# Four graph layers on one core: the last stage's two passes as one, a deeper gather ring in the segment maximum, and another engine to release adjacency slots

## The reference

```
xs, xd = x[src], x[dst]
reflection(a, b) = relu([a, b] @ W1.T) @ W2.T        # 32 -> 64 -> 16
F = I - 2 v v^T  with v = reflection / its norm      # one for (xs, xd), one for (xd, xs)
msg_s = coef * (-F_s^T F_d xd)   added to node src
msg_d = coef * (-F_d^T F_s xs)   added to node dst
out = relu(x - sum of msg_s by src - sum of msg_d by dst)
```

## Time and profile before

| | us |
|---|---|
| median of 3 runs | 8465.72 (8461.97 to 8473.73) |
| the profiled execution, its own time | 8461.1 |
| its span, first to last instruction | 8459.0 |

### The profile page before, as it was taken

How to read it: one execution, slowest core, us unless ns; L and a number is a source line. 1 busy time by engine, 2 the same in 40 slices (tenths; PEclk the granted TensorE clock), 3 DMA queues, 4 the chain that set the end, 5 groups by cost and what they waited for, 6 DMA issues and landing times. The chain is left out here.

```text
span 8459.0 us, 123102 instructions
## 1 busy us (share of the span) xinstructions
PE 5854.0 (69%) x33625; PEld 3950.5 (47%) x33626; DVE 6136.2 (73%) x12788; ACT 1635.2 (19%) x2872; POOL 4450.0 (53%) x4142
## 2 busy tenths in 40 slices
PE   3433333347444477777699999466559699999999
PEld 1333333236444455555455555255424366666555
DVE  5766666547333399999899999889900188888898
ACT  0011111001010144444222222034100022222000
POOL 0377767567777577777477777300000177777100
PEclk9999999955555599999899999677879755555899
DMA  2122222233111233333411111022065311111000
GB/s 97 32 52 53 52 51 52 43 108 70 38 36 38 37 79 80 80 80 79 54 44 43 43 44 43 13 94 99 31 253 205 148 31 32 32 32 32 3 0 1
DMA packets 487779, 514.79 MB, mean 61 GB/s; under 512 B 259365, under 2 KB 389805, under 8 KB 477106
## 3 DMA queue, kind: packets, MB, share of 16 engines
q1 hardware_dynamic: 344198, 446.65, 16.9%
q0 software_dynamic: 132160, 43.97, 6.5%
q10 hardware_dynamic: 11232, 21.73, 0.8%
HBM read 415.02 MB, written 95.99 MB: 60 GB/s over the span
## 5 line engine op out<-in xcount | busy, mean ns | idle before, releaser
L1257 POOL DMA_INDIRECT sh_ring<-node,sh_idx x832 | 856.8, 1030 | 1535.4 <-DVE sh_idx L1895 1277.6
L421 POOL DMA_INDIRECT slots<-rank_staged,rank_row_i x800 | 952.0, 1190 | 414.7 <-issue 210.1
L1507 POOL DMA_INDIRECT slots<-sm_rec,sm_row x832 | 900.9, 1083 | 361.8 <-issue 208.8
L1257 POOL DMA_INDIRECT mx_ring<-node,mx_idx x832 | 861.1, 1035 | 398.2 <-issue 239.5
L919 POOL DMA_INDIRECT mid_ring<-typed,mid_idx x832 | 873.5, 1050 | 258.7 <-issue 253.2
L401 PE MATMUL rank_found<-rank_next_sb,rank_hot_hi_t 25*125 25x128 f32 x1600 | 407.3, 431 | 840.3 <-ACT rank_next_sb L386 825.0
L1617 PE MATMUL sm_sums<-sm_both,sm_hot 128*128 128x512 f32 x1664 | 787.1, 595 | 0.4 <-issue 0.2
L401 PEld LDWEIGHTS rank_found<-rank_next_sb,rank_hot_hi_t 25*125 25x125 f32 x1600 | 353.6, 321 | 890.3 <-DVE rank_hot_hi_t L340 890.3
L1124 PE MATMUL mid_sums<-mid_ring,mid_hot_d 128*128 128x17 f32 x1664 | 391.7, 375 | 455.9 <-DMA mid_ring<-typed,mid_idx 443.5
L1124 PEld LDWEIGHTS mid_sums<-mid_ring,mid_hot_d 128*128 128x128 f32 x1664 | 383.3, 312 | 472.6 <-issue 472.6
L2135 PE MATMUL srl_sums<-srl_outer,srl_hot_lo 128*128 128x400 f32 x1664 | 560.9, 500 | 7.4 <-DVE srl_outer L2117 7.4
(11 more groups left out here) (403 smaller groups left out, 13634.0 us busy)
## 6 DMA issues: line engine op xcount, KB each, us to landing
strips<-near SPq DMA_DIRECT2D x76, 1600.0 KB, 10.8
mx_far<-far_row SPq DMA_DIRECT2D x208, 256.0 KB
rank_key_row<-key_rows SPq DMA_DIRECT2D x200, 244.1 KB
near<-adj_whole SPq DMA_DIRECT2D x175, 256.0 KB, 2.0
sm_low<-low_row SPq DMA_DIRECT2D x208, 128.0 KB
sh_low<-low_row SPq DMA_DIRECT2D x104, 256.0 KB, 3.3
feat_t<-mid_out ACTq DMA_DIRECT2D x104, 204.0 KB
mx_feat<-feat_t SPq DMA_DIRECT2D x208, 102.0 KB
```

Of the source, the lines that this page charges most:

```text
L421: pool.indirect_dma_start(m.slots, bass.IndirectOffsetOnAxis(ap=row_i[:, h, j:j + 1], axis=0), staged[:, h, j, :], None).then_inc(sent[h], 16)
L1257: pool.indirect_dma_start(ring[:, h, j, :], None, table, bass.IndirectOffsetOnAxis(ap=idx[:, h, j:j + 1], axis=0)).then_inc(part, 16)
L1507: pool.indirect_dma_start(m.slots2, bass.IndirectOffsetOnAxis(ap=row2[:, t:t + 1], axis=0), rec2[:, t, :], None).then_inc(ordered, 16)
```

## The change

The messages and the sums by source become one stage, `sheaf_messages`, of 52 turns of sixteen tiles (`MB`), rolled by a new helper `fours` over four turns. `to_sources` and `m.parts` are gone. The DVE one-hots of the node in its block are made in 16 bits with both operands in 16 bits, in pairs of tiles; the one for sources is widened to 32 bits by ACT (`widen`). The 32-bit product L2135 stays as it is, as `sources`, in two halves of eight tiles for each batch. `outer` now has one buffer for each half. The turned ends and the hidden layer go through PSUM in chunks of 512 columns, two buffers each. All gather indices are written at once, and the ring holds four batches; POOL's gathers are unrolled.

In the segment maximum the indices are written once and the ring holds four batches; PE's and ACT's loops cover four turns.

In the adjacency POOL loads the release counts, waits on `evac` and adds one to a new semaphore `freed` for each tile; PE waits on `freed` against a running count and loads eight table values a turn. `m.table` is laid out accordingly.

```diff
+MB = 16
...
+        @block.gpsimd
+        def _(pool):
+            def turn(q, h):
+                n = 2 * q + h
+                _, cleared_by = nc.values_load_multi_w_load_instructions(
+                    m.table[0:1, 1, bass.ds(n * BT, BT)], engines=[mybir.EngineType.Pool], min_val=0,
+                    max_val=(NB - 1) * (WIDTH_SLOTS + 1), skip_runtime_bounds_check_because=COUNTED)
+                for j in range(BT):
+                    pool.wait_ge(evac, cleared_by[j] & 511)
+                    pool.sem_inc(freed, 1)
+
+            batches(pool, total, 1, 1, turn)
+
...
                 _, at = nc.values_load_multi_w_load_instructions(
-                    m.table[0:1, bass.ds(n * BT, BT), :].rearrange("o t k -> o (t k)"), engines=[mybir.EngineType.PE], min_val=0,
+                    m.table[0:1, 0, bass.ds(n * BT, BT)], engines=[mybir.EngineType.PE], min_val=0,
                     max_val=(WIDTH_SLOTS - 1) * P, skip_runtime_bounds_check_because=COUNTED)
                 pe.wait_ge(hot_s, n + 1)
                 for j in range(BT):
-                    pe.wait_ge(evac, at[2 * j + 1] & 511)
+                    pe.wait_ge(freed, n * BT + j + 1)
                     for k in range(3):
-                        last = nc.tensor.matmul(sums[:, bass.ds(at[2 * j], P)], hot[:, h, j // 2, :, j % 2], heavy[:, h, k, j // 2, :, j % 2], start=False,
+                        last = nc.tensor.matmul(sums[:, bass.ds(at[j], P)], hot[:, h, j // 2, :, j % 2], heavy[:, h, k, j // 2, :, j % 2], start=False,
...
+def fours(eng, total, body):
+
+    for j in range(4):
+        body(0, j)
+    with eng.Fori(0, total - 2) as i:
+        for j in range(4):
+            body(i + 1, j)
+    for j in range(4):
+        body(total - 1, j)
+
...
     with ExitStack() as ctx:
         sb, ps, sem = makers(nc, ctx, "mx")
-        idx, ring = sb("idx", [P, 2, HB], I32), sb("ring", [P, 2, HB, W40])
+        idx, ring = sb("idx", [P, NT], I32), sb("ring", [P, DEEP, HB, W40])
...
         def _(pool):
-            gather(nc, m, pool, m.node40, idx, ring, idx_s, gathered, HB, HT // 2)
+            pool.wait_ge(idx_s, 1)
+            for n in range(HT):
+                if n >= DEEP:
+                    pool.wait_ge(held, n - DEEP + 1)
+                for j in range(HB):
+                    t = n * HB + j
+                    pool.indirect_dma_start(ring[:, n % DEEP, j, :], None, m.node40,
...
-                if inside(n + 2):
-
-                    dve.wait_ge(held, n + 1)
-                    indices(n + 2, h)
...
+                nc.scalar.copy(m.held[:, bass.ds(n * HB, HB), :], ring[:, k, :, 0:D]).then_inc(held, 1)
 
             def widened(n):
                 act.wait_ge(wide_s, n + 1)
...
-    total = NT // TB
...
+        idx, ring, low = sb("idx", [P, NT], I32), sb("ring", [P, DEEP, MB, HW]), sb("low", [P, 2, MB * P], FP16)
+        src_i, hi_i, lo_i = (sb(n, [P, NT], I32) for n in ("src_i", "hi_i", "lo_i"))
+        hi, real = sb("hi", [P, NT]), sb("real", [P, NT])
+        lo16, src16, iota = sb("lo16", [P, NT], BF16), sb("src16", [P, NT], BF16), sb("iota", [P, P, 2], BF16)
+        hot, hot_t = sb("hot", [P, 2, MB // 2, P, 2], BF16), sb("hot_t", [P, MB * P], BF16)
+        hot_s, hot_w, hot_hi = sb("hot_s", [P, MB // 2, P, 2], BF16), sb("hot_w", [P, 2, MB, P]), sb("hot_hi", [P, MB, NB])
+        outer = sb("outer", [P, 2, MB // 2, NB * D])
+        ends, ends_t, hid = sb("ends", [P, 2, MB, 2, D]), sb("ends_t", [2 * D, MB * P]), sb("hid", [P, MB * P])
...
+        xd, et_ps, hid_ps = ps("xd", [P, 512]), ps("et_ps", [2 * D, 2, 512]), ps("hid_ps", [P, 2, 512])
+        v_ps, sums, sums_f = ps("v_ps", [P, MB, 2 * D]), ps("sums", [P, 512]), ps("sums_f", [P, 512])
...
+            pool.wait_ge(idx_s, 1)
+            for n in range(total):
+                if n >= DEEP:
+                    pool.wait_ge(vec_s, n - DEEP + 1)
+                for j in range(MB):
+                    t = n * MB + j
+                    pool.indirect_dma_start(ring[:, n % DEEP, j, :], None, m.node20,
+                                            bass.IndirectOffsetOnAxis(ap=idx[:, t:t + 1], axis=0)).then_inc(gathered[n % DEEP], 16)
...
+
+            def far_hots(q, j):
+                n, h = 4 * q + j, j % 2
+                dve.wait_ge(loaded[h], (2 * q + j // 2 + 1) * 16)
                 wait(dve, xd_s, n)
                 nc.vector.tensor_scalar(hot_t[:, :], low[:, h], m.iota_col[:, 0:1], None, ALU.is_equal).then_inc(hot_t_s, 1)
...
+            def near_hots(n, h):
                 wait(dve, used, n - 1)
-                nc.vector.tensor_tensor(hot[:, h], slot_field(m, n * TB, TB, LO)[:, :, None].to_broadcast([P, TB, P]),
-                                        m.iota_row[:, None, :].to_broadcast([P, TB, P]), ALU.is_equal).then_inc(hot_s, 1)
...
+                nc.vector.tensor_tensor(hot[:, h], by_pairs(lo16, n), columns, ALU.is_equal).then_inc(hot_d_s, 1)
+                wait(dve, wide_s, 2 * n)
+                nc.vector.tensor_tensor(hot_s[:, :, :, :], by_pairs(src16, n), columns, ALU.is_equal).then_inc(hot_s_s, 1)
+
...
+                dve.wait_ge(v_s, 4 * n + 4)
+                link(nc.vector.tensor_tensor(flat(vec), v_ps[:, :, :], m.mlp_b2[:, None, :].to_broadcast([P, MB, 2 * D]), ALU.add))
                 link(nc.vector.tensor_tensor(sq[:, :, :, :], vec[:, :, :, :], vec[:, :, :, :], ALU.mult))
                 nc.vector.tensor_reduce(norm[:, :, :], sq[:, :, :, :], AX.X, ALU.add).then_inc(norm_s, 1)
                 if inside(n + 2, total):
-                    far_hots(q + 1, h)
+                    far_hots(q + (j + 2) // 4, (j + 2) % 4)
+                near_hots(n, h)
+                nc.vector.tensor_tensor(hot_hi[:, :, :], hi[:, bass.ds(n * MB, MB)][:, :, None].to_broadcast([P, MB, NB]),
+                                        m.iota_row[:, None, 1:NB + 1].to_broadcast([P, MB, NB]), ALU.is_equal).then_inc(chain, 1)
+                c[0] = c[0] + 1
...
                 if inside(n + 2, total):
-                    gather_ends(q + 1, h)
-
-            for h in range(2):
-                indices(h, h)
+                    gather_ends(q + (j + 2) // 4, (j + 2) % 4)
+                for k in range(2):
+                    t = slice(k * MB // 2, (k + 1) * MB // 2)
+                    wait(dve, spent, 2 * n - 1 + k)
+                    nc.vector.tensor_tensor(outer[:, k].rearrange("q t (s d) -> q t s d", d=D),
+                                            both[:, t, 0, :][:, :, None, :].to_broadcast([P, MB // 2, NB, D]),
+                                            hot_hi[:, t, :, None].to_broadcast([P, MB // 2, NB, D]), ALU.mult).then_inc(outer_s, 1)
...
+            def turned(n, c):
+                act.wait_ge(et_s, 4 * n + c + 1)
+                nc.scalar.copy(ends_t[:, c * 512:(c + 1) * 512], et_ps[:, c % 2, :]).then_inc(ends_t_s, 1)
+
+            def hidden(n, c):
+                act.wait_ge(hp_s, 4 * n + c + 1)
+                nc.scalar.activation(hid[:, c * 512:(c + 1) * 512], hid_ps[:, c % 2, :], ACT.Relu, bias=m.mlp_b1[:, 0:1]).then_inc(hid_s, 1)
...
+            def widen(n, h, k):
+                if k == 0:
+                    act.wait_ge(hot_s_s, n + 1)
+                    wait(act, spent, 2 * n - 2)
+                nc.scalar.copy(hot_w[:, h, k * MB // 2:(k + 1) * MB // 2, :].rearrange("q (a t) c -> q a t c", t=2),
+                               hot_s[:, k * MB // 4:(k + 1) * MB // 4, :, :].rearrange("q a c t -> q a t c")).then_inc(wide_s, 1)
...
                 act.wait_ge(norm_s, n + 1)
                 nc.scalar.activation(norm[:, :, :], norm[:, :, :], ACT.Sqrt).then_inc(root_s, 1)
-                if inside(n + 1, total):
-                    network(n + 1)
-                act.wait_ge(three_s, n + 1)
-                nc.scalar.copy(m.parts[:, bass.ds(n * TB, TB), :], both[:, h, :, 0, :]).then_inc(kept_s, 1)
-
-            network(0)
-            batches(act, total, 1, 1, turn)
+                if more:
+                    turned(n + 1, 0)
+                    turned(n + 1, 1)
+                    hidden(n + 1, 0)
+                    turned(n + 1, 2)
+                    hidden(n + 1, 1)
+                    turned(n + 1, 3)
+                widen(n, h, 0)
+                if more:
+                    hidden(n + 1, 2)
+                widen(n, h, 1)
+                if more:
+                    hidden(n + 1, 3)
...
+            def sources(n, h, k):
+                pe.wait_ge(outer_s, 2 * n + k + 1)
+                pe.wait_ge(wide_s, 2 * n + k + 1)
+                for j in range(MB // 2):
+                    last = nc.tensor.matmul(sums_f[:, 0:NB * D], hot_w[:, h, k * MB // 2 + j, :], outer[:, k, j, :], start=False, stop=True,
+                                            skip_group_check=True)
+                last.then_inc(spent, 1)
+
+            def turn(q, j):
+                n, h = 4 * q + j, j % 2
```

(43 more changed lines are left out.)

297 lines of the change are left out of this document (133 added, 164 removed).

## The result

| | us |
|---|---|
| before, median of 4 runs | 8463.84 (8461.23 to 8473.73) |
| after, median of 4 runs | 8633.15 (8623.0 to 8652.89) |
| ratio | 1.0201, interval 1.0181 to 1.0221 |
| profiled execution after: its own time, its span | 8652.89, 8651.1 |

What follows compares the result with a forecast made beforehand. PE was taken to bound both sheaf stages; merged, steps a to f sum to 34.7 us a turn, the stage +120 us. With segment maximum -79 and adjacency -18, 8461.1 became 8484, forecast as 8490 us, range 8400 to 8590.

Steps and rivals of the forecast that it cites:

- a: Merged turn's start: DVE's operations to the norms, then ACT's root and first copy, before PE's hidden layer starts; 3.0 us.
- f: Merged turn's end: DVE writes outer's second half only after PE's sources have counted it spent; 3.8 us.
- b: Merged turn, PE at 1.2 GHz up to the sources: hidden chunks, transposes, far-end products, vectors; 13.6 us.
- c: Merged turn, first half of PE's sources, eight tiles, the clock rising after 3.6 us; 7.2 us.
- d: Merged turn, PE's two groups of vectors between the halves of the sources; 1.7 us, or 3.2 if the clock isn't up.
- e: Merged turn, second half of PE's sources; 5.4 us.
- the rule of the Trainium skill: Rival in the merged stage: PE's busy time raises the clock 3.6 us into b; turn 27.9 us, kernel 8135, chance 0.05.
- the small parts bring nothing: Rival: the segment maximum and adjacency edits gain nothing; kernel 8490 + 80 = 8570 us, chance 0.07.
- Segment maximum, -79 forecast: Segment maximum: DVE's index write and waits for late gathers go; 208 turns of 5.40 us, 1123 us, -79 (-50 to -95).
- POOL's floor: Segment maximum: least turn POOL's gathers allow, 1.32 us a tile, 5.3 us for four; at the most -95 us.
- Adjacency, -18 forecast: Adjacency: halved table loads cut PE's late starts, the detour over POOL costs some; -18 us, from +15 to -45.
- issue time halved: Sign to look for in the adjacency: PE's issue time at the weight loads, 272.4 us before, should be halved.

Runs made afterwards that it cites:

- The experiment with full rows: Changed kernel with the hidden layer's weights and turned ends held in 128 rows, 96 of them zero: 8326.69 us, ratio 0.9838.
- the other kernels: Four kernels measured side by side with the changed segment maximum's code: that stage took 1152 to 1157 us in all.
- the kernel with both edits: Changed kernel with hidden-layer products over 128 rows and outer's second half written behind the next turn's norms: 8076.68 us, ratio 0.9547.
- the pieces: The kernel with both edits, each half of outer written by four DVE instructions of 800 elements: ratios 0.9647, 0.9647, 0.9434 on disturbed chips.

## Why the prediction was wrong

- **Which engine binds, and the order of the turn: right.** DVE's 22.3 us were 22.2, the waits a and f stand where they were put, and moving one of them gained 6.8 us a turn. It was no bar to the merge but a mistake in its order.
- **b, 13.6 forecast, 15.5 measured: mis-sized.** I took a hidden chunk as half the distance of two that followed each other, 1.85 us. In the merged order each stands between other products and takes 2.0, four times. Vectors took 1.83 instead of 1.6, twice; part of that is a reading, since I took the starts of weight loads, and the products' own starts in the old turn give (7214.55 - 7211.13) / 2 = 1.7. The far ends took 2.08 instead of 1.3, the largest error (0.8). The 0.64 a batch was no misreading; the products' own starts in the old turn say the same:

```profile
7210.48 0.81 PE L2020 MATMUL sh_xd<-wide,sh_hot_t 128*128 x24
7211.13 3.60 PE L2042 MATMUL sh_v_ps<-mlp,sh_hid 128*128 128x32 f32 x16
```

  What failed is doubling it. In the merged turn the first 26 of the 48 products also start 0.027 us apart; the rest come with pauses of about 0.1 us, 0.8 us in all. PE's program works out block addresses in register operations (FUSED_REGOPS in the trace), by their count one for two products, and 0.125 us apart. Nine of them are done when the products start, in the old order as in the merged one. The old batch needs three more, which come in time; the double batch needs fifteen more, and 15 x 0.125 = 1.9 us is nearly the 2.08 that the group takes. The transposes took 0.1 more. 0.6 + 0.5 + 0.8 + 0.1 is the missing 1.9 us, within rounding.
- **c, 7.2 forecast, 8.3 measured: mis-sized.** The clock came up after 5.7 us of sources, not 3.6. One rise was taken as the delay of all; it is a range. Steps d, e and f held to 0.1 us.
- **The price of a turn.** 52 x (37.24 - 34.7) = 132 us of the 139 that the stage missed by; filling and draining took 7 more. My range for the turn, 34.1 to 36.3, let only d, a and an earlier clock vary. None of the terms that failed had a bound of its own.
- **Rivals.** None came about. The clock did not come up in b, so the rule of the Trainium skill (TensorE: Matmul & The Clock Gate, What's actually happening), by which busy time releases it, gives 8135 where 8633 was measured: PE was busy without a break from 7417.6 on, and the clock came at 7438.8. The experiment with full rows says what the row of busy time leaves out: a PE that was no busier (85% against 88%) had 0.83 when its hidden products filled the rows. (The sum of the rival "the small parts bring nothing" leaves out the adjacency's 18 us; it should read 8587, not 8570.)
- **Segment maximum, -79 forecast, -20 in the profile, -53 in the kernel with the merge undone (1205 to 1152).** The mechanism held: the old waits for indices are gone, and POOL waits for next to nothing in the changed stage:

```profile
L1359 POOL DMA_INDIRECT mx_ring<-node,mx_idx x832 | 888.5, 1068 | 323.5 <-issue 248.4 <-DVE mx_idx L1388 69.3 <-ACT held L1399 5.9
```

  (The 69.3 lie ahead of the first gather.) Two terms were mis-sized. One is POOL's floor, 1.32 us a tile plus 0.1 a turn: the gathers follow each other with 0.30 us between, (888.5 + 248.4) / 832 = 1.37 us a tile, and the first 200 turns take 5.50 us each, where they took 5.66 before. In the other kernels it is 1.33 a tile and 5.34 a turn. The other is one pace for all turns. Near the end of the stage transfers of features come late to PE while the DMA engines are 91% busy (4040 to 4082; 34% in mid-stage): from the end of the 201st batch's gathers to the end of the stage it took 69 us before and 80 after. 200 x 0.16 - 11 is the 20 us of the profile, and 200 x 0.32 - 8 the 55 of the kernel with the merge undone. Nothing is hidden behind a deeper ring when the gathers themselves are the bound.
- **Adjacency, -18 forecast, -46 measured.** The gain lies at the far end of my range (-45), not where I put it. Every turn is now DVE's 3.22 us. PE's timeline before, then after (start, us):

```profile
5711.01 2.74 PE L679 MATMUL adj_sums<-adj_heavy,adj_hot 128*128 128x128 bf16 x24 [1.72 <-DVE adj_heavy L641]
5714.13 1.83 PE L679 MATMUL adj_sums<-adj_heavy,adj_hot 128*128 128x128 bf16 x24 [0.38 <-DVE adj_heavy L641]
5717.82 2.72 PE L679 MATMUL adj_sums<-adj_heavy,adj_hot 128*128 128x128 bf16 x24 [1.86 <-DVE adj_heavy L641]
```
```profile
5710.10 1.84 PE L694 MATMUL adj_sums<-adj_heavy,adj_hot 128*128 128x128 bf16 x24 [1.41 <-POOLq L677]
5713.35 1.81 PE L694 MATMUL adj_sums<-adj_heavy,adj_hot 128*128 128x128 bf16 x24 [1.41 <-DVE adj_heavy L643]
```

  Before, every other turn's 24 products took 2.7 us in this stretch, at half the clock; after, all take 1.8, and the granted clock is 0.98 where it was 0.81. I read the excess as load time and as waits for ACT, and did not look at the clock. The forecast sign "issue time halved" was wrong (276 us, as before), so the loads are not what was gained. Why the clock no longer falls is not settled: whether the detour over GpSimd does it, or the shorter work on PE's registers, was not separated.

## What to carry over

Before two stages are merged, ask which engine binds each: if it is the same one, merging saves nothing but the waits and the clock, and each new wait costs in full. Give every term of a serial sum its own bound, taken in the neighbourhood in which it will run, since a product alone between others took 2.0 us where two in a row took 1.85 each, and 48 small ones took more than twice what 24 did. And when two stages begin to overlap, look for operations that never ran beside each other before: here the long DVE write beside GpSimd's gathers set the next bound.

## What the runs showed of the hardware

- **A gather waits for the DVE instruction that runs.** One that starts beside a 3.49 us operation of two tensors takes up to 4.27 us and ends 0.82 us behind it at the median (98 of 124 in the kernel with both edits; the 26 that started within 0.043 us of its start were not held). Beside pieces of 0.9 us it takes at most 1.76, alone 0.94. With the pieces, 1 of 832 still waited for two DVE instructions in a row (3.14 us, in the first of three runs).
- **PE's register operations can hold small products.** One for two products, 0.125 us apart: a group of 48 pauses for 0.8 us behind its first 26 products (2.08 us in all; 3.3 in the turn shown of the kernel with both edits, where none of the 24 was done ahead); groups of 24, 0.65 us each, and of 12 hardly pause.
- **PE's busy share does not tell the clock.** It was 0.50 with PE busy from 7417.6 to 7438.8 (1.2 GHz, where 1.00 is 2.4). Zero rows added to the hidden layer's products (431 of PE's 1735 us in the stage) went with a mean of 0.83 instead of 0.68. With both edits it fell from 1.00 behind 3.3 us of far-end products; with these spread out, the mean of the stage with pieces was 0.89 instead of 0.83.
- **The rise is not at a fixed distance**: it came 3.6 us into the sums by source at one place and 5.7 at another.
- **The same kernel can take 11% longer elsewhere.** The kernel before took 8461 us on one chip and 9413 to 9486 on four others. Stages with gathers got longer there (the segment maximum, its code as before, went from 1207 to 1459 and 1486 us), the adjacency (629 in all three) not at all. A change that adds slack to the gathers can be slower on the one and faster on the other.
